# Offset attention in a two-layer decoder: outputs of two batches at a time, with gated mixtures kept in the buffer of the queries

## The chip, the cores and the metric

The kernel runs on one core of a Trainium2 chip. The metric is the device time of one execution in microseconds; of the kernel before there are three runs. TensorE is called PE here, VectorE DVE, ScalarE ACT, GpSimd POOL, and SyncE (which only starts transfers) SP.

## The reference

A decoder of two layers works on 16 batches of 112 tokens with 256 features: attention with future taps, cross attention, a mixture of experts, then offset attention, causal cross attention and a quantised perceptron. The change touches offset attention alone. Of the normalised input it makes queries, keys and values for 16 heads of 16 features, and for each allowed offset between query and key

```python
for i, o in enumerate(OFFSETS):
    qk = jnp.einsum('bhnd,bhnd->bhn', q, _shift(k, o))
    lg = qk * inv * (1.0 + qs[..., i]) + pos_bias[i][None, :, None]
    lg = jnp.where(pos[None, None, :] >= o, lg, NEG)
...
p = jax.nn.softmax(logits, axis=-1)
...
out = out * if_gain[None, :, None, None]
gate = jax.nn.sigmoid(x @ gate_w.T + gate_b)
return out_flat * gate @ out_w.T + out_b
```

The result is added to the residual stream `xT`. All arithmetic is float32.

## The kernel before

The stages follow each other, each with a block of instruction streams of its own, one per engine, written in the order in which they run; semaphores join them. The stage before this one left the queries of all batches in `qz_all` (`[P, 2, C, TOK]`: two variants, two halves, 1792 tokens), the gates in `gateT`, and the factors `1 + q . embedding` in DRAM.

`token_attention` (line 1352) serves three stages; in this one `offset` is true. Every engine loops over n = 0 to 17. Iteration n holds the front half of batch n and the back half of batches n-1 and n-2:

- PE (from line 1600): `scores(n)` (L1499), into PSUM banks 0 to 3; `turn(n-1, 0)` and `turn(n-1, 1)` (L1508), which transpose the probabilities; a norm's matmul (`beside.pe`, L256 or L273, bank 6) in iterations 7, 8, 11, 12, 15, 16; `turn` 2 and 3 and the products with the values, `mix` (L1523, bank 7); `values(n)` (L1471); `mix(n-1, 3)`; the keys of the next group of four batches (`project`, L1465) in iterations 1, 2, 5, 6, 9, 10, and those of the next stage (`project_cross`, L1578) in 13 to 15; then `output(n-2)` (L1539, bank 6).
- DVE (from line 1956): four `multiply` (L1851, scores times factors), the bias additions of two of the four groups of heads (L1856), a norm's centring (L261), four row maxima (L1863), the values (L1839), `spread_denominators(n-1)` (L1912), `add_output(n-2)` (L1922), then a norm's pair sum (L269), the queries of the next stage (L1831), a norm's scaling (L285) and sum (L252), where there are any.
- ACT (from line 1752): four copies of turned probabilities (L1721), the exponentials (L1727, eight small ones, and L1732, two large ones), `copy_mix(n-1)` (L1739) between them, keys (L1676), and the logarithm and exponential that invert the denominators (L1712, L1716).
- POOL (from line 2074): `normalise(n-2)` (L2040), two bias additions (L2045), two additions of the row maximum (L2050), `gate(n-1)` (L2032).
- SP fetches the factors of batch n when those of n-2 are used.

A mixture passes from bank 7 to `mixT` (ACT), times the gate to `gmixT` (POOL), times the inverted denominators in place (POOL), into the output's matmul (PE), and to `xT` with the bias (DVE). `mixT` and `gmixT` have two buffers here; the two other attention stages have four of `mixT` and already make the outputs of two batches at a time (`output_of_two`, L1548; `add_two`, L1945). Batches 14 and 15 go by `output_of_last` (L1557) in every stage. `x.after(At(n))` is the count that the semaphore x has after batch n; it starts four batches high, so that the first waits pass.

Of the kernel before, what the change touches and what calls it, by code (L numbers as in the profile page):

```python
# [12 lines left out]
ALU = mybir.AluOpType  # L13
# [3 lines left out]
P = 128  # L17
NB, T, D = 16, 112, 256
C = D // P
# [4 lines left out]
NG = H // HG  # L24
PADW = NG * P
FUT = 4
G = 448
# [1324 lines left out]
def token_attention(nc, kind, stage, psum, const, w, hT, accT, beside, ready, next_weights, ctxT=None, qz_all=None, gateT=None, skewed=None, startup=None, folded=None, big=None, spare=None, room=None, stored=None, perceptron=None, ups_ahead=None, weights=None, cross=None):  # L1352
# [9 lines left out]
    future, offset, causal = kind == "future", kind == "offset", kind == "causal"  # L1362
    ident, identb, maskb = const["ident"], const["identb"], const["maskb"]
    NV = 3 if future else 2
    with Scope(nc, stage, reuse=True) as s:
        NM = 2 if offset else 4
        mixT = qz_all[:, 0, 0].rearrange("p (u t) -> p u t", t=G) if causal else s.sb("mixT", [P, NM, G])
        if offset:
            gmixT = s.sb("gmixT", [P, 2, G])
        kT = cross.kT if causal else s.sb("kT", [P, 2, 2, G])  # L1370
# [4 lines left out]
        NR = 1 if offset else 2  # L1375
        rden = qz_all[:, 1, 0, 0:NR * G].rearrange("p (u t) -> p u t", u=NR) if causal else s.sb("rden", [P, NR, G])
        wt = w.at
# [32 lines left out]
        banks_free = factored if offset else shifted  # L1410
        out_mixT = gmixT if offset else mixT

# [40 lines left out]
        def _(pe):  # L1453
# [76 lines left out]

            def output(n):
                if offset:
                    pe.wait_ge(gained.sem, NG)
                beside.wait_bank(pe, n + 2)
                pe.wait_ge(*added.after(At(n - 1)))
                pe.wait_ge(*normed.after(At(n)))
                for m in range(C):
                    for g in range(NG):
                        mm = nc.tensor.matmul(psum[:, 6, m * T:(m + 1) * T], wt["wo"][:, g, m * P:(m + 1) * P], out_mixT[:, n % 2, g * T:(g + 1) * T], start=g == 0, stop=g == NG - 1)  # L1539
                mm.then_inc(projected.sem, 1)  # L1540

            def output_of_two(n):
                wait_norm_read(n + 1, n + 3)
                pe.wait_ge(*added.after(At(n // 2 - 1)))
                pe.wait_ge(*normed.after(At(n + 1)))
                for m in range(C):
                    for g in range(NG):
                        mm = nc.tensor.matmul(psum[:, 6, 2 * m * T:2 * (m + 1) * T], wt["wo"][:, g, m * P:(m + 1) * P], out_mixT[:, n % NM:n % NM + 2, g * T:(g + 1) * T], start=g == 0, stop=g == NG - 1)  # L1548
                mm.then_inc(projected.sem, 1)

            def output_of_last(n):

                bank = 4 + n % 2
                pe.wait_ge(*normed.after(At(n)))
                for m in range(C):
                    for g in range(NG):
                        mm = nc.tensor.matmul(psum[:, bank, m * T:(m + 1) * T], wt["wo"][:, g, m * P:(m + 1) * P], out_mixT[:, n % NM, g * T:(g + 1) * T], start=g == 0, stop=g == NG - 1)  # L1557
                mm.then_inc(projected.sem, 1)
# [41 lines left out]
            for n in range(NB + 2):  # L1600
# [18 lines left out]
                if beside.halves(n):  # L1619
                    pe.wait_ge(*added.after(At(n - 3 if offset else (n - 4) // 2)))  # L1620
                    beside.pe(pe, n, 6)
# [29 lines left out]
                if causal and n >= NB:  # L1651
                    for k in range(2):
                        pe.wait_ge(*shifted.after(At(NB - 1), 2 * (n - NB) + k))
                        weights.turn(pe, 2 * (n - NB) + k)
                if last and now and offset:
                    output(n - 2)
                elif n >= NB:
                    output_of_last(n - 2)
                elif not offset and n >= 3 and n % 2:
                    output_of_two(n - 3)  # L1660

        @block.scalar
        def _(act):
# [70 lines left out]
            def copy_mix(n):  # L1734
                if offset and n == 0:
                    act.wait_ge(*stored.after(At(NB - 1)))
                act.wait_ge(*mixed.after(At(n), NG - 1))
                act.wait_ge(*projected.after(At(n - 2 if offset else n // 2 - 2)))
                nc.scalar.copy(mixT[:, n % NM], psum[:, 7, 0:G]).then_inc(mix_copied.sem, 1)  # L1739
# [70 lines left out]
        def _(dve):  # L1810
# [102 lines left out]

            def add_output(n):
                dve.wait_ge(*projected.after(At(n)))
                if future:
                    x = accT[:, :, n * T:(n + 1) * T]
                    nc.vector.tensor_tensor(x, x, psum[:, 6, 0:C * T].rearrange("p (c t) -> p c t", c=C), ALU.add).then_inc(added.sem, 1)
                    return
                for c in range(C):  # L1920
                    x = accT[:, c, n * T:(n + 1) * T]
                    a = nc.vector.scalar_tensor_tensor(x, psum[:, 6, c * T:(c + 1) * T], wt["bo"][:, c:c + 1], x, ALU.add, ALU.add)  # L1922
                a.then_inc(added.sem, 1)

            def add_of_last(n):
                bank = 4 + n % 2
                dve.wait_ge(*(projected.after(At(n)) if offset else projected.after(At(NB // 2 - 1), n - (NB - 2))))
                if future:
                    x = accT[:, :, n * T:(n + 1) * T]
                    nc.vector.tensor_tensor(x, x, psum[:, bank, 0:C * T].rearrange("p (c t) -> p c t", c=C), ALU.add).then_inc(added.sem, 1)  # L1930
                    return
                for c in range(C):
                    x = accT[:, c, n * T:(n + 1) * T]
                    a = nc.vector.scalar_tensor_tensor(x, psum[:, bank, c * T:(c + 1) * T], wt["bo"][:, c:c + 1], x, ALU.add, ALU.add)
                a.then_inc(added.sem, 1)
# [20 lines left out]
            for n in range(NB + 2):  # L1956
# [43 lines left out]
                for name, g, m in pieces(n):  # L2000
                    if n < NB and name == "q":
                        take_queries(g, m, 5)
                if last and now and offset:
                    add_output(n - 2)
                    beside.dve_pair_now(dve, n)
                    if n in CROSS_AT and CROSS_AT[n][0] == "q":
                        take_cross_queries(CROSS_AT[n][1], 5)
# [5 lines left out]
                if offset and beside.sums(n):  # L2013
                    dve.wait_ge(*added.after(At(n - 2)))
                    beside.dve_sum(dve, n)

        @block.gpsimd
        def _(pool):
# [8 lines left out]
            def gate(n):  # L2027
                u = n % 2
                pool.wait_ge(*mix_copied.after(At(n)))
                pool.wait_ge(*projected.after(At(n - 2)))  # L2030
                m, gm = (x[:, u].rearrange("p (g t) -> p g t", g=NG) for x in (mixT, gmixT))
                nc.gpsimd.tensor_tensor(gm, m, gateT[:, :, n * T:(n + 1) * T], ALU.mult).then_inc(gated.sem, 1)  # L2032

            def normalise(n):
                u = n % 2
                if offset:
                    pool.wait_ge(*gated.after(At(n)))
                pool.wait_ge(*inverted.after(At(n)))
                x = out_mixT[:, n % NM]
                nc.gpsimd.tensor_tensor(x, x, rden[:, n % NR], ALU.mult).then_inc(normed.sem, 1)  # L2040

# [1156 lines left out]
```

## Time and profile before

| | us |
|---|---|
| median of 3 runs | 1714.85 (1712.42 to 1718.21) |
| the profiled execution | 1716.57 |
| its span | 1714.6 |
| PE busy | 1568.2 (91%) |
| DVE busy | 892.1 (52%) |
| ACT busy | 812.9 (47%) |
| POOL busy | 371.5 (22%) |
| offset attention | about 1329 to 1485 of the span |

Busy is the time in which the engine executes at least one instruction; the rest is waiting or issue. The shares are means over the whole span, and stages differ: over most of the span DVE, ACT and POOL wait for PE, and in offset attention all four are busy most of the time. A timeline row gives the start, the duration and the instruction, then in brackets how long the engine sat idle before it and whose instruction ended that wait; equal instructions that follow each other are merged to one row (x2). A shuffle (L1912) comes once in each iteration from 1 to 16, so the starts of its rows cut the stage into batches.

### The profile page before, as it was taken

The page shows a single profiled execution, that of the slowest core. Times are in us where ns is not written, and L with a number is a line of the kernel's source. Part 1 is how long each engine was busy: PE and PEld are TensorE (multiplying, and loading weights), DVE is VectorE, ACT ScalarE, POOL GpSimd, SP SyncE. Part 2 cuts the span into 40 slices and gives each one's busy share as a digit, 9 for nine tenths or more (in the row PEclk, how much of TensorE's full clock was granted, in tenths as well). Part 3 has the DMA queues.
Part 4 walks back from the last instruction along what each step waited for, and adds up shares of the span by engine and source line. Part 5 has one row for each costly group of instructions (what it writes and reads, how often), then busy time and mean ns, then how long its engine had stood idle before and what let it go on. Part 6 is the DMA issues. An engine that isn't in the chain of part 4 may idle for free. (4 is left out here: it accounts for less than half of the span.)

```text
span 1714.6 us, 34568 instructions
## 1 busy us (share of the span) xinstructions
PE 1568.2 (91%) x13646; PEld 1024.7 (60%) x13646; DVE 892.1 (52%) x1863; ACT 812.9 (47%) x1585; POOL 371.5 (22%) x337
## 2 busy tenths in 40 slices
PE   8899999999799999999799999999787899899965
PEld 3455555555356666656565999999344666566642
DVE  4566666511555565555242211111273889667758
ACT  4355555533144544455431222222254788556666
POOL 0012222221100010000028300000721777311222
PEclk9999999999899999999789999999999899999988
DMA  7000000010200000000043799997379443000001
GB/s 264 1 1 2 1 1 2 22 34 1 85 20 11 20 20 20 20 11 2 14 162 126 227 328 329 326 326 238 94 193 219 118 95 88 12 12 12 2 1 44
DMA packets 148051, 150.16 MB, mean 88 GB/s; under 512 B 69890, under 2 KB 135106, under 8 KB 147890
## 3 DMA queue, kind: packets, MB, share of 16 engines
q1 hardware_dynamic: 144818, 140.60, 26.9%
q0 software_dynamic: 3072, 7.34, 1.4%
q8 instruction: 109, 1.79, 0.5%
q14 instruction: 52, 0.43, 0.1%
HBM read 120.40 MB, written 27.53 MB: 86 GB/s over the span
## 5 line engine op out<-in xcount | busy, mean ns | idle before, releaser
L2506 DVE TENSOR_TENSOR masked<-masked 128x512 f32<-128x512 f32 x70 | 49.8, 712 | 200.9 <-ACT masked L2408 200.9
L958 DVE CUSTOM_DVE_ANT_0 x_unused<-psum,masked 112x439 f32<-112x439 f32 x256 | 141.8, 610 | 20.3 <-PE psum L781 19.6
L896 ACT ACTIVATE x_probs<-psum,key_mask 125x448 f32<-125x448 f32 x192 | 106.1, 635 | 77.4 <-PE psum L801 77.4
L2349 PEld LDWEIGHTS psum<-mix_xb,mix_up 128*128 128x128 f32 x1120 | 130.6, 192 | 2.1 <-issue 0.4
L2349 PE MATMUL psum<-mix_xb,mix_up 128*128 128x128 f32 x1120 | 130.7, 275 | 0.0
L2359 PE MATMUL psum<-mix_down,masked 128*128 128x256 f32 x560 | 127.0, 380 | 0.1
L1477 PE MATMUL psum<-fold_full,hT 128*112 128x512 f32 x256 | 113.8, 597 | 1.3 <-DVE fold_part L1872 1.3
L2359 PEld LDWEIGHTS psum<-mix_down,masked 128*128 128x128 f32 x560 | 103.5, 190 | 13.4 <-DVE masked L2506 0.4
L1721 ACT COPY masked<-psum 112x448 f32<-112x448 f32 x128 | 63.8, 530 | 60.6 <-PE psum L1508 60.3
L781 PE MATMUL psum<-x_kT,x_qz 32*112 32x439 f32 x512 | 88.4, 591 | 3.2 <-DVE x_kT L943 3.2
L2408 ACT ACTIVATE masked<-psum 128x512 f32<-128x512 f32 x70 | 41.8, 597 | 97.1 <-PE psum L2349 97.1
L1032 POOL TENSOR_TENSOR x_mixT<-x_mixT,x_rden 128x448 f32<-128x448 f32 x16 | 18.2, 1140 | 316.1 <-ACT x_rden L902 316.1
L801 PE MATMUL psum<-x_qmax,x_kT 32*125 32x112 f32 (+1 forms) x2048 | 81.4, 285 | 4.5 <-DVE x_qmax L966 3.8
L801 PEld LDWEIGHTS psum<-x_qmax,x_kT 32*125 32x125 f32 (+1 forms) x2048 | 66.7, 179 | 29.6 <-issue 20.8
L1508 PE MATMUL psum<-ident,second_result 112*112 112x112 f32 x512 | 70.2, 270 | 13.4 <-ACT masked L1721 9.4
L1477 PEld LDWEIGHTS psum<-fold_full,hT 128*112 128x112 f32 x256 | 44.1, 177 | 61.4 <-issue 58.9
L815 PEld LDWEIGHTS psum<-x_probs,x_v 125*32 125x32 f32 (+1 forms) x2048 | 47.5, 110 | 46.8 <-issue 26.3
L285 DVE TENSOR_TENSOR hT<-hT,sq 128x896 f32<-128x896 f32 x24 | 26.4, 1098 | 85.7 <-ACT sq L279 85.7
L1508 PEld LDWEIGHTS psum<-ident,second_result 112*112 112x112 f32 x512 | 50.9, 136 | 32.4 <-issue 23.6
L1115 POOL DMA_INDIRECT hrow<-slots_y,slot x16 | 15.6, 973 | 248.8 <-POOLq L148 245.3
L815 PE MATMUL psum<-x_probs,x_v 125*32 125x112 f32 (+1 forms) x2048 | 64.1, 264 | 4.7 <-ACT x_probs L896 4.6
L2414 ACT COPY mix_result<-psum 128x256 f32<-128x256 f32 x35 | 13.0, 372 | 99.1 <-PE psum L2359 99.1
(338 smaller groups left out, 3277.5 us busy)
## 6 DMA issues: line engine op xcount, KB each, us to landing
mix_up<-in_moe_up SPq DMA_DIRECT2D x35, 1024.0 KB
mix_down<-in_moe_down SPq DMA_DIRECT2D x35, 1024.0 KB
offset_rows<-join_rows SPq DMA_DIRECT2D x16, 784.0 KB, 5.7
hrow<-offset_rows SPq DMA_DIRECT2D x16, 784.0 KB, 5.2
x_ctx<-in_ctxT SPq DMA_DIRECT2D x16, 375.0 KB, 3.1
slots_x<-masked SPq DMA_DIRECT2D x1, 4480.0 KB, 21.4
mix_rows<-slots_x SPq DMA_DIRECT2D x35, 128.0 KB, 3.4
slots_y<-mix_result SPq DMA_DIRECT2D x35, 128.0 KB, 3.5
```

Source lines behind the costliest of these rows:

```text
L781: nc.tensor.matmul(psum[0:T, bank(*use), 0:KEYS], qz[rows, n // BATCHES_OF % 2, e, m, t:t + T], kT[rows, n % 3, m, e], start=True, stop=Tr ...
L801: mm = nc.tensor.matmul(psum[0:keys_of, bank(*use), k * T:(k + 1) * T], kT[rows, n % 3, m, e, c * CHUNK:c * CHUNK + keys_of], qmax[rows, k ...
L815: mm = nc.tensor.matmul(psum[32 * k:32 * k + 32, 7, g * T:(g + 1) * T], v[0:rows, n % 2, c, HG * g + k, :], probs[0:rows, 4 * (c % 2) + 2 ...
L896: nc.scalar.activation(probs[0:rows, 4 * (c % 2) + r], psum[0:rows, bank("tile", n, 4 * c + r), 0:G].rearrange("p (k t) -> p k t", k=4), A ...
L958: nc.vector.tensor_tensor_reduce(unused[:, at], psum[0:T, at, 0:KEYS], masked[0:T, n * KEYS:(n + 1) * KEYS], -1.0, -3.0 * NEG, ALU.add, AL ...
L1477: mm = nc.tensor.matmul(psum[0:T, bank, :], hT[:, c, n * T:(n + 1) * T], taps, start=c == 0, stop=c == C - 1)
L1508: mm = nc.tensor.transpose(psum[0:T, 4 + i % 2, k * T:(k + 1) * T], probs[:, n % 2, HG * i + k], ident[0:T, 0:T])
L1721: nc.scalar.copy(turned[:, i], psum[0:T, 4 + i % 2, 0:G].rearrange("p (k t) -> p k t", k=HG)).then_inc(copied.sem, 1)
L2349: mm = nc.tensor.matmul(psum[:, 2 * u + half, m * BLOCK:(m + 1) * BLOCK], e_up[:, w, c, (half * H4 + m) * P:(half * H4 + m + 1) * P], xb[: ...
L2359: mm = nc.tensor.matmul(psum[:, 6 + u, 0:D], e_hidden[:, u, m, :], e_down[:, w, m, :], start=m == 0, stop=m == M8 - 1)
L2408: nc.scalar.activation(e_relu[:, half], psum[:, 2 * (k % 2) + half, :].rearrange("p (m t) -> p m t", m=H4), ACT.Relu).then_inc(relu_done.s ...
L2506: nc.vector.tensor_tensor(e_hidden[:, u, half * H4:(half + 1) * H4], e_relu[:, half], e_relu[:, half], ALU.mult).then_inc(hidden_ready.sem, 1)
```

## The change

For the offset stage `NM`, the number of `mixT` buffers, goes from two to four. `gmixT` is no longer a buffer of its own: it is a view of `qz_all`, and the gated mixture of batch n takes the columns of the queries of batch n, once the scores of that batch are made. `output` and `add_output`, which did one batch in each iteration, are gone; `output_of_two` and `add_two` do two batches in odd iterations from 3 to 15. The waits follow: `copy_mix` waits for the gating and the shuffle of the batch four before, `gate` for the scores, and the norms' waits on `added` count pairs.

```diff
-        NM = 2 if offset else 4
+        NM = 4
...
-            gmixT = s.sb("gmixT", [P, 2, G])
+            gmixT = qz_all[:].rearrange("p e m t -> p (e m) t")
...
+        def mixed_heads(g, n, count):
+            if offset:
+                return gmixT[:, g, n * T:(n + count) * T]
+            return mixT[:, n % NM:n % NM + count, g * T:(g + 1) * T]
...
-            def output(n):
-                if offset:
+            def output_of_two(n):
+                if offset and n == 0:
                     pe.wait_ge(gained.sem, NG)
-                beside.wait_bank(pe, n + 2)
-                pe.wait_ge(*added.after(At(n - 1)))
-                pe.wait_ge(*normed.after(At(n)))
-                for m in range(C):
-                    for g in range(NG):
-                        mm = nc.tensor.matmul(psum[:, 6, m * T:(m + 1) * T], wt["wo"][:, g, m * P:(m + 1) * P], out_mixT[:, n % 2, g * T:(g + 1) * T], start=g == 0, stop=g == NG - 1)
-                mm.then_inc(projected.sem, 1)
-
-            def output_of_two(n):
                 wait_norm_read(n + 1, n + 3)
                 pe.wait_ge(*added.after(At(n // 2 - 1)))
                 pe.wait_ge(*normed.after(At(n + 1)))
                 for m in range(C):
                     for g in range(NG):
-                        mm = nc.tensor.matmul(psum[:, 6, 2 * m * T:2 * (m + 1) * T], ..., out_mixT[:, n % NM:n % NM + 2, g * T:(g + 1) * T], ...)
+                        mm = nc.tensor.matmul(psum[:, 6, 2 * m * T:2 * (m + 1) * T], ..., mixed_heads(g, n, 2), ...)
...
                 if beside.halves(n):
-                    pe.wait_ge(*added.after(At(n - 3 if offset else (n - 4) // 2)))
+                    pe.wait_ge(*added.after(At((n - 4) // 2)))
...
-                if last and now and offset:
-                    output(n - 2)
-                elif n >= NB:
+                if n >= NB:
                     output_of_last(n - 2)
-                elif not offset and n >= 3 and n % 2:
+                elif n >= 3 and n % 2:
                     output_of_two(n - 3)
...
                 act.wait_ge(*mixed.after(At(n), NG - 1))
-                act.wait_ge(*projected.after(At(n - 2 if offset else n // 2 - 2)))
+                if offset:
+                    act.wait_ge(*gated.after(At(n - NM)))
+                    act.wait_ge(*spread.after(At(n - NM)))
+                else:
+                    act.wait_ge(*projected.after(At(n // 2 - 2)))
...
+                if offset and now and n >= 3 and n % 2:
+                    add_two(n - 3)
                 if last and now and offset:
-                    add_output(n - 2)
                     beside.dve_pair_now(dve, n)
...
                 if offset and beside.sums(n):
-                    dve.wait_ge(*added.after(At(n - 2)))
+                    dve.wait_ge(*added.after(At((n - 3) // 2)))
...
             def gate(n):
-                u = n % 2
                 pool.wait_ge(*mix_copied.after(At(n)))
-                pool.wait_ge(*projected.after(At(n - 2)))
-                m, gm = (x[:, u].rearrange("p (g t) -> p g t", g=NG) for x in (mixT, gmixT))
+                pool.wait_ge(*scored.after(At(n), NG - 1))
+                m, gm = mixT[:, n % NM].rearrange("p (g t) -> p g t", g=NG), gmixT[:, :, n * T:(n + 1) * T]
                 nc.gpsimd.tensor_tensor(gm, m, gateT[:, :, n * T:(n + 1) * T], ALU.mult).then_inc(gated.sem, 1)
...
-                x = out_mixT[:, n % NM]
-                nc.gpsimd.tensor_tensor(x, x, rden[:, n % NR], ALU.mult).then_inc(normed.sem, 1)
+                x = gmixT[:, :, n * T:(n + 1) * T] if offset else mixT[:, n % NM]
+                nc.gpsimd.tensor_tensor(x, x, rden[:, n % NR].rearrange("p (g t) -> p g t", g=NG) if offset else rden[:, n % NR], ALU.mult).then_inc(normed.sem, 1)
```

The rest of the diff drops `add_output` and the counts of `projected` by single batches.

## Rows read from the trace of the kernel before

**Rows 1.** Windows view, the repeating part: us; busy (count) of PE, PEld, DVE, ACT, POOL; clock; DMA.

```profile
1350.89:1469.18 118.29, 108.09 (x1346) 79.78 (x1345) 106.01 (x207) 96.93 (x236) 91.05 (x79) 1.00 0.36 84
```

**Rows 2.** PE timeline, next stage (pairs): start us, us, instruction; a pair's output, its successor.

```profile
1518.41 3.19 PE L1548 MATMUL psum<-qz_all,weights 128*128 128x224 f32 x16
1521.43 0.92 PE L1493 MATMUL psum<-maskb,identb 112*112 112x448 bf16 x4
```

**Rows 3.** PE timeline, iterations 4 to 6, cut.

```profile
1363.03 0.56 PE L1508 MATMUL psum<-ident,second_result 112*112 112x112 f32 x4 [1.48 <-ACT masked L1721]
...
1375.55 1.93 PE L1539 MATMUL psum<-a_gmixT,weights 128*128 128x112 f32 x16
1377.42 1.05 PE L1499 MATMUL psum<-a_kT,qz_all 32*112 32x112 f32 x32
...
1379.87 0.57 PE L1508 MATMUL psum<-ident,second_result 112*112 112x112 f32 x4 [0.49 <-ACT masked L1721]
...
1383.12 1.77 PE L1465 MATMUL psum<-hT,weights 128*128 128x448 f32 x4
1384.73 1.93 PE L1539 MATMUL psum<-a_gmixT,weights 128*128 128x112 f32 x16
```

**Rows 4.** DVE timeline, offset attention, cut (L1912 STREAM_SHUFFLE opens each period).

```profile
1350.89 0.66 DVE L1912 STREAM_SHUFFLE a_rden<-a_mixT 128x448 f32<-128x448 f32 x1
...
1360.07 0.66 DVE L1912 STREAM_SHUFFLE a_rden<-a_mixT 128x448 f32<-128x448 f32 x1
...
1361.09 1.14 DVE L1851 SCALAR_TENSOR_TENSOR second_result<-hrow,psum 112x448 f32<-112x448 f32 x2
1362.15 0.62 DVE L1856 TENSOR_TENSOR second_result<-second_result,weights 112x448 f32<-112x448 f32 x1
...
1364.28 1.08 DVE L1856 TENSOR_TENSOR second_result<-second_result,weights 112x448 f32<-112x448 f32 x1
...
1367.73 0.66 DVE L1912 STREAM_SHUFFLE a_rden<-a_mixT 128x448 f32<-128x448 f32 x1
...
1376.38 0.66 DVE L1912 STREAM_SHUFFLE a_rden<-a_mixT 128x448 f32<-128x448 f32 x1
...
1378.49 1.15 DVE L1851 SCALAR_TENSOR_TENSOR second_result<-hrow,psum 112x448 f32<-112x448 f32 x2 [0.39 <-PE psum L1499]
1379.56 1.51 DVE L1856 TENSOR_TENSOR second_result<-second_result,weights 112x448 f32<-112x448 f32 x1
...
1385.56 0.66 DVE L1912 STREAM_SHUFFLE a_rden<-a_mixT 128x448 f32<-128x448 f32 x1
...
1387.31 0.63 DVE L252 TENSOR_TENSOR sq<-xT 128x448 f32<-128x448 f32 x1
...
1395.97 0.65 DVE L1912 STREAM_SHUFFLE a_rden<-a_mixT 128x448 f32<-128x448 f32 x1
...
1413.24 0.66 DVE L1912 STREAM_SHUFFLE a_rden<-a_mixT 128x448 f32<-128x448 f32 x1
...
1422.41 0.66 DVE L1912 STREAM_SHUFFLE a_rden<-a_mixT 128x448 f32<-128x448 f32 x1
...
1469.18 0.66 DVE L1912 STREAM_SHUFFLE a_rden<-a_mixT 128x448 f32<-128x448 f32 x1
...
1471.15 1.38 DVE L1831 TENSOR_SCALAR gateT<-psum,weights,half 128x448 f32<-128x448 f32 x2
```

**Rows 5.** POOL timeline, two rows of iterations 4 and 6.

```profile
1363.73 2.63 POOL L2045 TENSOR_TENSOR second_result<-second_result,weights 112x448 f32<-112x448 f32 x2
...
1379.45 1.14 POOL L2040 TENSOR_TENSOR a_gmixT<-a_gmixT,a_rden 128x448 f32<-128x448 f32 x1 [1.25 <-ACT a_rden L1716]
```

**Rows 6.** ACT timeline, iteration 4.

```profile
1364.92 2.35 ACT L1727 ACTIVATE second_result<-second_result,a_rowmax 112x112 f32<-112x112 f32 x8
```

**Rows 7.** Groups by line, 1335 to 1485: busy us, mean ns, idle before.

```profile
L1922 DVE SCALAR_TENSOR_TENSOR xT<-psum,weights,xT 128x112 f32<-128x112 f32 x28 | 8.0, 326 | 3.7 <-PE psum L1539 3.7
```

**Rows 8.** DVE timeline, next stage: the addition of a pair.

```profile
1521.63 0.81 DVE L1945 SCALAR_TENSOR_TENSOR xT<-psum,weights,xT 128x224 f32<-128x224 f32 x2 [3.76 <-PE psum L1548]
```

More of the change, by code:

```diff
@@ L1410, in token_attention @@
         banks_free = factored if offset else shifted
-        out_mixT = gmixT if offset else mixT
+        def mixed_heads(g, n, count):
+            if offset:
+                return gmixT[:, g, n * T:(n + count) * T]
+            return mixT[:, n % NM:n % NM + count, g * T:(g + 1) * T]
         def factor_load(sp, n):
@@ L1547, in output_of_two @@
                     for g in range(NG):
-                        mm = nc.tensor.matmul(psum[:, 6, 2 * m * T:2 * (m + 1) * T], wt["wo"][:, g, m * P:(m + 1) * P], out_mixT[:, n % NM:n % NM + 2, g * T:(g + 1) * T], start=g == 0, stop=g == NG - 1)
+                        mm = nc.tensor.matmul(psum[:, 6, 2 * m * T:2 * (m + 1) * T], wt["wo"][:, g, m * P:(m + 1) * P], mixed_heads(g, n, 2), start=g == 0, stop=g == NG - 1)
                 mm.then_inc(projected.sem, 1)
@@ L1556, in output_of_last @@
                     for g in range(NG):
-                        mm = nc.tensor.matmul(psum[:, bank, m * T:(m + 1) * T], wt["wo"][:, g, m * P:(m + 1) * P], out_mixT[:, n % NM, g * T:(g + 1) * T], start=g == 0, stop=g == NG - 1)
+                        mm = nc.tensor.matmul(psum[:, bank, m * T:(m + 1) * T], wt["wo"][:, g, m * P:(m + 1) * P], mixed_heads(g, n, 1), start=g == 0, stop=g == NG - 1)
                 mm.then_inc(projected.sem, 1)
@@ L1912, in spread_denominators @@
                 nc.vector.stream_shuffle(rden[:, n % NR], mixT[:, n % NM], [HD] * 32).then_inc(spread.sem, 1)
[L1914 to L1923, printed above, removed]
             def add_of_last(n):
                 bank = 4 + n % 2
-                dve.wait_ge(*(projected.after(At(n)) if offset else projected.after(At(NB // 2 - 1), n - (NB - 2))))
+                dve.wait_ge(*projected.after(At(NB // 2 - 1), n - (NB - 2)))
                 if future:
```

## The prediction

> **What bounds the kernel now.** I read the share of each engine first, then the stretches, then the timelines of offset attention. Only the part from the second to the last `stream_shuffle` of a denominator repeats: 118.29 us, with PE busy for 108.09 (91%), DVE 106.01 (90%), ACT 96.93 (82%), POOL 91.05 (77%) at full clock [rows 1]. The change touches one stage of 8% of the span, and no engine there has slack for all of a saving to be hidden or for all of it to be paid out. So the order within a batch decides, and I follow it from one shuffle (L1912) to the next. I call the stretch that the shuffle of iteration n opens period n, and give times in it from that shuffle's start.
>
> Periods last 9.18 us (n=2), 7.66 (3), 8.65 (4), 9.18 (5), 10.41 (6), 17.27 (7 and 8 together), 9.17 (9) and 46.76 (10 to 14) [rows 4]. They have a common form. Let m be the start of the first `multiply` (L1851). In period 3 it is 1.02, and the second L1856 took 1.08 us beside a POOL operation where the first, alone, took 0.62: 7.66 - 1.02 - 0.47 = 6.17. In period 5 m is 2.11 and the first L1856 took 1.51: 2.11 + 6.17 + 0.90 = 9.18 [rows 4]. So a period is m + 6.17 + what L1856 loses to POOL (+1.0 where a norm's centring is in it).
>
> Two things set m. DVE cannot start before the shuffle is issued, some 0.6; PE must have the scores: they start when the output ends, and L1851 follows 1.07 after their start (1377.42 to 1378.49) [rows 3, 4].
>
> There is a floor too. PE's third turn waits for an ACT copy, 2.96 into a period without keys (1363.03) and 3.49 into one with keys (1379.87) [rows 3]; the eight exponentials after it run without a gap in iteration 4 [rows 6], so ACT's chain ends 4.70 after that turn (1367.73 - 1363.03), and DVE's ends at the same time. A period is therefore not under 7.66, or 8.19 with keys. POOL's two bias additions, 2.63 us together [rows 5], are nearly as late.
>
> **The change, part by part.**
>
> *PE.* Fourteen outputs of one batch become seven of two. One takes 1.87 us to the next instruction (1375.55 to 1377.42) [rows 3]; one of two takes 3.02 (1518.41 to 1521.43) in the next stage, with equal shapes [rows 2]. Each pair saves 2 x 1.87 - 3.02 = 0.72 of PE, 5.0 us in seven. But it is no even saving: an even iteration loses 1.87 of PE work, an odd one gains 1.15, just ahead of the scores for which DVE waits.
>
> *DVE.* Two additions of some 0.57 become one of 0.81 per pair [rows 7, 8]. In odd periods it runs while PE computes the scores, in even ones DVE starts at 0.6 anyway; its 0.3 is inside m.
>
> *Even periods.* No output, so the scores are there before the shuffle and m falls to 0.6.
> - Period 2: POOL's L2040 stands at 3.07 with keys (1379.45) [rows 5], past the first L1856 at 1.7. The floor binds: 8.19 for 9.18, a gain of 0.99.
> - Period 4: the floor without keys, 7.66 for 8.65: 0.99.
> - Period 6: L252 stands before L1851, at 1.75 and 0.55 long [rows 4]. m falls from 2.30 to 1.15, and the L2040 that lengthened the first L1856 is now behind it, some 0.2: 1.37. Periods 10 and 14 have the same form: 1.37 each.
> - Periods 8 and 12: m is held by DVE's norm scale (about 1.1), and ends where it did: nothing.
>
> *Odd periods.* The output starts when the fourth mixture (and the keys) is through: 3.25 after the third turn (1379.87 to 1383.12), and 1.61 later with keys (to 1384.73) [rows 3]. m = its start + 3.02 + 1.07.
> - Period 3: the output starts at 3.49 + 3.25 - 8.19 = -1.45; m = 2.64; the period 8.81, no L1856 in POOL's way (POOL's bias addition then waits for the multiply): a loss of 1.15.
> - Period 5: 2.96 + 3.25 + 1.61 - 7.66 = +0.16; m = 4.25; 10.42: a loss of 1.24.
> - Periods 7 and 11: PE ends the output at about 0.7, DVE has the shuffle, the addition and a sum of squares to do until 2.2; the same first L1856 as now waits for L2040: under 0.1 of loss, taken as nothing.
> - Period 9: output from -0.9 to 2.15; m = 3.2; 9.39, for L1856 comes behind L2040 and no longer waits for it: a loss of 0.22. Period 13 comes to the same 9.39. Periods 10 to 14 last 46.76, and after the change by the above 9.04 + 17.27 + 9.39 + 9.04 = 44.74 (10 and 14 as period 6, 11 and 12 as 7 and 8, 13 as 9), a gain of 2.02.
>
> *The tail.* In iteration 15 DVE's cross queries end at 1471.15 + 1.38, 3.35 after the last shuffle [rows 4], and PE's next turn waits for them. With the output from -0.7 to 2.3, the addition of two, the sum of squares and the two L1831 behind it end at 5.3. Everything from there to the stage's end is one chain: a loss of 1.9. (If DVE's part stayed hidden it would be 0; it cannot be more than 3.02.)
>
> *Mixtures.* Four buffers instead of two, and `copy_mix` waits for POOL's gating and the shuffle of four batches ago instead of for an output: never late, before or after. POOL's gate now writes, and L2040 reads and writes, four runs of 112 with the stride of a row of `qz_all`. The gate reads `gateT` with that stride today; the trace has no strided write on POOL. The elements are the same, so it costs no less than 0; from above the nearest row is L2045, 1.31 each in a pair against L2040's 1.14 [rows 5]: 0.17 x 2 x 14 = 4.8 us if all of it were on the path. I take 0: a row of L2040 with a plain layout is the nearest, and it has slack before it. The gate's new wait, on scores of an iteration ago, is always met; behind it on POOL only the next normalisation stands. SP's loads wait for `factored` alone, and no DVE row waits for them here. The last output, now of batches 12 and 13, still needs the normalisation of 13 only.
>
> Sum: -0.99 (2) + 1.15 (3) - 0.99 (4) + 1.24 (5) - 1.37 (6) + 0 (7, 8) + 0.22 (9) - 2.02 (10 to 14) + 1.9 (tail) = **-0.9 us**. The profiled execution took 1716.57 (span 1714.6), so it becomes 1715.7; against the median of 1714.85 that is **1714.0**. A change under 0.3% (5.1 us) cannot be told from none here.
>
> **A rule to weigh.** L1856 has two inputs in SBUF and took 1.51 where POOL's L2040 had started 0.11 before it, and 0.62 alone [rows 4, 5]. The Trainium skill ("SBUF — State Buffer", section "SBUF: two separate sides") calls the ports that VectorE and GpSimd share an exclusive lock: who starts first has them for the whole instruction, the other fully blocks. The trace agrees for the loser on DVE's side (the row ends 0.48 after L2040 does). By this rule each L1856 whose start moves by a few tenths can turn from free to blocked, which is the second rival.
>
> **Rivals.**
> - *PE is the bound* (faster). If the odd periods' longer output were covered, PE's 5.0 us would come out whole: 1714.85 - 5.0 = 1709.8. For it: PE is the busiest engine and waits seldom [rows 1]. Against: DVE waits for scores right behind outputs, and the even iterations leave PE idle at ACT's copy [rows 3].
> - *POOL takes the port first in odd periods* (slower). With m late, POOL has long done L2040, and its two bias additions are released by DVE's second and fourth multiply, just as the two L1856 are issued behind them. If POOL were first, each L1856 would lose what the one of period 5 loses to L2040, 0.90. It decides from the point where L2045 starts before L1856, in periods 3, 5, 9 and 13, where nothing else is slack: 8 x 0.90 = 7.2, and 7.2 - 0.9 = +6.3: 1721.2. For it: both wait for the same multiply. Against: DVE issues L1856 without a wait (1362.15, right behind the two multiplies that began at 1361.09), and POOL has a semaphore to pass first [rows 4].
> - *The floor is higher* (same). If periods 2 and 4 kept their length (POOL's bias additions ending later as DVE comes to them earlier), 2.0 of the gain would be missing: 1716.0.
> - *The change does not do what it says:* with the output of two not at full rate, e.g. 2 x 1.87, odd periods would lose 0.7 more each, 1718; the next stage shows 3.02, so this has little.
>
> **How the numbers follow.** The forecast 0.63, the higher floor 0.14, PE as the bound 0.11, POOL's port 0.08, slow outputs or strided writes 0.04. Faster than 0.3%: the first rival, which lies at that edge and which I count there with what shorter L1856 would add, 0.11; slower: the second, 0.08; the same: 0.81. For the forecast alone 1712 to 1716. The range takes in the first rival and the strided writes (1714.0 + 4.8), and leaves out POOL's port: 1709.5 to 1719.
>
> **What would show it.** Periods must alternate: about 8.2, 8.8, 7.7, 10.4, 9.0, 9.0, 8.3, 9.4 for n = 2 to 9, where they now take 9.2, 7.7, 8.7, 9.2, 10.4, 17.3 for two, 9.2. L1548 in this stage 3.02 from start to successor, seven times; m of 0.6 in even periods, 2.6 and over in odd ones; DVE waiting for L1548 in odd periods only; the stage from the last shuffle to its end longer by 1.9. Wrong if even periods stay at 8.6 or more, if L1856 is long behind a pair's output, if L2040 or L2032 exceed 1.2, or if the total moves by over 5 us.

## The result, and the profile after

The changed kernel is slower. Against the kernel before on the same chip its time is a ratio of 1.0063 (95% interval 1.005 to 1.0076): 1729.36 us median of 15 runs against 1716.74 of 15, where 1714.0 and no measurable change were forecast. The profiled execution took 1726.35, its span is 1724.6 with PE busy for 1574.8 and a mean granted clock of 0.958 (before: 1714.6, 1568.2, 0.965). Chips differ by several microseconds, so whole times are compared below by the ratio to the kernel before on the same chip; periods come from the one profiled execution of each kernel. Three executions of the experiments, which took 1.5 to 5 times as long as the others of their kernel, are left out of the ratios.

Cut at the shuffles as before [rows 4], the stage gives:

| period n | 2 | 3 | 4 | 5 | 6 | 7 + 8 | 9 | 10 to 12 | 13 | 14 | 2 to 14 | 15 |
|---|---|---|---|---|---|---|---|---|---|---|---|---|
| before | 9.18 | 7.66 | 8.65 | 9.18 | 10.41 | 17.27 | 9.17 | 27.70 | 8.65 | 10.42 | 118.29 | 9.18 |
| predicted | 8.19 | 8.81 | 7.66 | 10.42 | 9.04 | 17.27 | 9.39 | 26.31 | 9.39 | 9.04 | 115.5 | |
| after | 9.01 | 9.76 | 9.45 | 11.62 | 10.42 | 17.28 | 10.96 | 28.40 | 11.53 | 10.42 | 128.85 | 11.32 |

(10 to 12 predicted: 9.04 + 17.27.) The repeating part is 10.6 us longer, period 15 another 2.1. What follows the last shuffle is 0.9 longer up to the start of the stage's last addition (6.16 for 5.28), and 2.4 up to the next stage's first operation on DVE (11.67 for 9.24). That makes some 15 us in this pair of traces, where the ratio gives 10.8 (8.6 to 13.0); the rest of the difference is not located. The spans differ by 10.0 only because the part ahead of the stage, which the change does not touch, was 5.2 us shorter in the execution after (the stage's first multiply starts at 1322.00 for 1327.16).

The first view to open is the windows view, here periods 2, 4, 5, 8, 12 and 13 of the kernel after: length, busy time and count of PE, PEld, DVE, ACT and POOL, then the granted clock, the DMA share and GB/s.

```profile
1346.06:1355.07 9.01, 6.96 (x71) 4.55 (x65) 6.97 (x15) 7.30 (x19) 7.30 (x7) 0.81 0.56 127
1364.83:1374.28 9.45, 7.19 (x53) 4.31 (x52) 7.36 (x13) 6.78 (x18) 7.36 (x7) 0.64 0.55 124
1374.28:1385.90 11.62, 11.29 (x109) 7.78 (x107) 7.29 (x15) 7.41 (x19) 6.29 (x6) 1.00 0.15 39
1405.27:1413.60 8.33, 5.98 (x50) 3.62 (x48) 7.96 (x16) 6.67 (x18) 6.44 (x7) 0.80 0.33 78
1443.93:1452.96 9.03, 6.68 (x48) 3.82 (x46) 8.04 (x14) 6.76 (x18) 7.16 (x7) 0.62 0.40 95
1452.96:1464.49 11.53, 11.20 (x109) 7.77 (x107) 7.28 (x15) 7.40 (x19) 6.29 (x6) 1.00 0.07 16
```

In the kernel before the clock of this whole part is 1.00 [rows 1]. Here it falls in four even periods (2, 4, 8 and 12), and again in period 15 (0.85). The PE timeline of the end of iteration 4 and of iteration 5 shows what PE did before, and what it costs:

```profile
1364.55 0.98 PE L1513 MATMUL psum<-ident,second_result 112*112 112x112 f32 x8 [0.38 <-DVE a_v L1837]
1367.80 0.97 PE L1513 MATMUL psum<-ident,second_result 112*112 112x112 f32 x4 [2.26 <-ACT masked L1715]
1368.69 0.60 PE L1528 MATMUL psum<-masked,a_v 112*32 112x112 f32 x8
1369.23 1.00 PE L1513 MATMUL psum<-ident,second_result 112*112 112x112 f32 x4
1370.15 0.98 PE L1528 MATMUL psum<-masked,a_v 112*32 112x112 f32 x16
1371.06 2.05 PE L1476 MATMUL psum<-weights,hT 128*112 128x256 f32 x4
1373.04 0.60 PE L1528 MATMUL psum<-masked,a_v 112*32 112x112 f32 x8
1373.57 2.12 PE L1470 MATMUL psum<-hT,weights 128*128 128x448 f32 x4
1375.53 3.19 PE L1544 MATMUL psum<-qz_all,weights 128*128 128x224 f32 x16
1378.65 1.05 PE L1504 MATMUL psum<-a_kT,qz_all 32*112 32x112 f32 x32
```

The same place in the kernel before, cut:

```profile
1370.69 0.57 PE L1508 MATMUL psum<-ident,second_result 112*112 112x112 f32 x4 [0.48 <-ACT masked L1721]
...
1372.57 1.12 PE L1471 MATMUL psum<-weights,hT 128*112 128x256 f32 x4
```

With no output in iteration 4, PE waits 2.26 us for ACT's copy, where the kernel before waited 0.48. Four transposes then take 0.97 (0.57 before) and the values 2.05 (1.12 before): about half the speed, the level of 1.2 GHz. The keys and with them the output start late, though the output itself takes 3.12 (1375.53 to 1378.65), near the 3.02 predicted. DVE waits at both ends, as its timeline shows for period 4's end and period 5:

```profile
1373.15 0.42 DVE L1837 TENSOR_TENSOR a_v<-psum,weights 112x256 f32<-112x256 f32 x1 [1.35 <-PE psum L1476]
...
1374.28 0.66 DVE L1910 STREAM_SHUFFLE a_rden<-a_mixT 128x448 f32<-128x448 f32 x1
1378.76 0.81 DVE L1932 SCALAR_TENSOR_TENSOR xT<-psum,weights,xT 128x224 f32<-128x224 f32 x2 [3.81 <-PE psum L1544]
1379.72 1.15 DVE L1849 SCALAR_TENSOR_TENSOR second_result<-hrow,psum 112x448 f32<-112x448 f32 x2 [0.15 <-PE psum L1504]
1380.79 0.62 DVE L1854 TENSOR_TENSOR second_result<-second_result,weights 112x448 f32<-112x448 f32 x1
```

m is 5.44 (1379.72 - 1374.28) instead of 4.25, and the first L1854 (the L1856 of before) is free, 0.62. So are both L1854 of periods 3, 9 and 13 (0.61 to 0.62): the second rival, POOL taking the port in odd periods, did not happen.

A second thing stands in periods 6, 10 and 14, which lost nothing and gained nothing. DVE and, below it, POOL of the kernel after, period 6:

```profile
1385.90 0.66 DVE L1910 STREAM_SHUFFLE a_rden<-a_mixT 128x448 f32<-128x448 f32 x1
1386.46 1.74 DVE L252 TENSOR_TENSOR sq<-xT 128x448 f32<-128x448 f32 x1
1388.12 1.14 DVE L1849 SCALAR_TENSOR_TENSOR second_result<-hrow,psum 112x448 f32<-112x448 f32 x2
1389.18 1.41 DVE L1854 TENSOR_TENSOR second_result<-second_result,weights 112x448 f32<-112x448 f32 x1
```

```profile
1386.57 1.14 POOL L2019 TENSOR_TENSOR qz_all<-a_mixT,gateT 128x448 f32<-128x448 f32 x1
1388.97 1.14 POOL L2027 TENSOR_TENSOR qz_all<-qz_all,a_rden 128x448 f32<-128x448 f32 x1 [1.26 <-ACT a_rden L1710]
```

L252 now follows the shuffle directly, meets POOL's gate (L2019) and takes 1.74 for the 0.63 of [rows 4]; then L1854 starts 0.21 behind L2027 and takes 1.41. Each ends 0.48 or 0.49 after the POOL operation does (1388.20 for 1387.71, 1390.59 for 1390.11). POOL's own operations keep their 1.14: the strided writes cost nothing that shows.

### The profile page after: what moved, and what is told of

The parts are those of the page before. It is cut to its first block and busy times, and to the rows that moved or that the text cites. A ratio compares the mean times of both kernels' runs of the same rounds, so it can differ in the third digit from the quotient of the medians.

```text
span 1724.6 us, 34321 instructions
## 1 busy us (share of the span) xinstructions
PE 1574.8 (91%) x13534; PEld 1023.6 (59%) x13534; DVE 890.7 (52%) x1849; ACT 811.8 (47%) x1585; POOL 370.8 (22%) x337
## 5 line engine op out<-in xcount | busy, mean ns | idle before, releaser
L2346 PEld LDWEIGHTS psum<-mix_down,masked 128*128 128x128 f32 x560 | 103.5, 190 | 13.3 <-DVE masked L2493 0.4
L1513 PE MATMUL psum<-ident,second_result 112*112 112x112 f32 x512 | 73.9, 278 | 21.0 <-ACT masked L1715 13.1
L1470 PE MATMUL psum<-hT,weights 128*128 128x448 f32 x120 | 55.1, 591 | 7.2 <-issue 4.4
```

Source lines behind the costliest of these rows:

```text
L1470: mm = nc.tensor.matmul(psum[:, bank, 0:G], wt["w" + name][:, c, m * P:(m + 1) * P], src, start=c == 0, stop=c == C - 1)
L1513: mm = nc.tensor.transpose(psum[0:T, 4 + i % 2, k * T:(k + 1) * T], probs[:, n % 2, HG * i + k], ident[0:T, 0:T])
L2346: mm = nc.tensor.matmul(psum[:, 6 + u, 0:D], e_hidden[:, u, m, :], e_down[:, w, m, :], start=m == 0, stop=m == M8 - 1)
```

## The experiments

Each was timed beside the kernel before, on the same chip. A filler below is a matmul whose result nobody reads.

**e1_buffers** takes the kernel before and changes only the buffers.

```diff
-        NM = 2 if offset else 4
+        NM = 4
-            gmixT = s.sb("gmixT", [P, 2, G])
+            gmixT = qz_all[:].rearrange("p e m t -> p (e m) t")
 ... the new waits of copy_mix and gate; output(n) and add_output(n) stay
```

> The kernel before with the new buffers alone: four mixT, the gated mixture in the columns of qz_all, the new waits; outputs still one batch in each iteration. My theory (the slowdown is from PE's idle time in even iterations and the slower clock that follows, and from DVE operations that now run into POOL's gate) expects the time of before, within 0.1%, clock 1.00 in the stage and periods of 7.7 to 10.4 us as before. If POOL's strided writes or the new waits cost, L2032 and L2040 exceed 1.14 us and the time is up to 5 us longer.

Ratio 1.0002 (0.9987 to 1.0017), and the repeating part 118.62 us for 118.29. The buffers and waits cost nothing that shows; the time is in the outputs' new order. One period of it (7) had a clock of 0.82 and 9.35 us, after a wait of 1.74 of PE; the kernel before has the same wait (1.73) and kept 1.00.

**e2_filler** gives PE something to do in its waits. (The wait for `gained` moves from the first output to a place ahead of the first fillers.)

```diff
+                    if offset and now and n in (3, 5, 9, 13):      # after turn(n - 1, 1)
+                        for k in range(4 if n == 3 else 8):
+                            nc.tensor.matmul(psum[:, 6, G:G + 64], wt["wo"][:, k % NG, 0:P], wt["wo"][:, k % NG, 0:64], start=True, stop=True)
```

> The changed kernel with matmuls of no use (64 columns into an unused part of bank 6) where PE waits for ACT's copies: four in iteration 3, eight in 5, 9 and 13. Clock theory: in the changed kernel's trace the granted clock is 0.81, 0.64, 0.80 and 0.62 in periods 2, 4, 8 and 12, after waits of 1.0 to 2.4 us, and matmuls take 1.8 times as long; with PE kept busy the clock stays near 1.00, periods 2 and 4 fall to about 8.2 and 7.7, 5, 9 and 13 to 10.4, 9.4 and 9.4, in all 6 to 9 us less than the changed kernel. Rival (the longer output just before the scores is the cost by itself): the clock may rise, but the total stays within 1 us of the changed kernel, or grows by what the fillers take (up to 1.7 us each in four places).

Ratio 1.0022 (1.0004 to 1.004) for 1.0063: two thirds of the loss are gone, though PE has more to do. The clock is 1.00 in periods 4 to 15, and periods 4, 5, 9 and 13 are 7.65, 10.54, 9.44 and 9.44 us (after: 9.45, 11.62, 10.96, 11.53; predicted: 7.66, 10.42, 9.39, 9.39). Period 2 kept a clock of 0.68 and took 9.88 us, where about 8.2 was expected: PE had waited 1.06 us ahead of these fillers, for ACT's keys.

**e5_filler_all** adds four fillers between the first two turns of iteration 3, and eight there in iteration 16, behind waits that keep them off a bank still being read.

```diff
                     turn(n - 1, 0)
+                    if offset and n == 3:
+                        pe.wait_ge(gained.sem, NG)
+                    if offset and n == NB and True:
+                        pe.wait_ge(*added.after(At(6)))
+                    if offset:
+                        for k in range({3: 4, NB: 8}.get(n, 0)):
+                            nc.tensor.matmul(psum[:, 6, G:G + 64], ...)
```

> The changed kernel with fillers where the clock still fell in e2_filler: in iteration 3 four between the first two turns (PE waits 1.06 us there for ACT's keys) and four after them, eight after the turns of 5, 9 and 13, and eight in iteration 16 between the first two turns (PE waits 2.8 us for DVE's queries). Clock theory: 1.00 in every period; 2 and 3 fall from 9.9 and 10.4 (e2_filler) to about 8.2 and 8.8 as the prediction had them, the rest stays as in e2_filler; 2 to 4 us below e2_filler, so within 0.1% of the kernel before. Rival (periods 2 and 3 are slow for another reason, a late start of the stage): the clock rises and they stay at 9.9 and 10.4.

Ratio 1.0016 (1.0003 to 1.003), where 0.1% at most was expected. Periods 2, 4, 5, 8, 12 and 13 in the windows view, to be read against the six rows of after:

```profile
1343.21:1351.38 8.17, 7.82 (x90) 6.23 (x85) 6.88 (x15) 7.20 (x19) 6.92 (x7) 1.00 0.63 142
1360.42:1368.06 7.64, 7.13 (x72) 5.23 (x71) 7.28 (x13) 6.67 (x18) 6.67 (x7) 1.00 0.57 139
1368.06:1378.61 10.55, 10.22 (x107) 7.21 (x105) 7.29 (x17) 7.42 (x19) 6.97 (x7) 1.00 0.22 53
1397.97:1406.30 8.33, 7.73 (x72) 5.64 (x70) 7.96 (x14) 6.78 (x18) 6.46 (x7) 1.00 0.34 81
1435.10:1443.42 8.32, 7.72 (x72) 5.63 (x70) 7.95 (x14) 6.77 (x18) 6.45 (x7) 1.00 0.33 79
1443.42:1452.88 9.46, 9.13 (x103) 6.30 (x101) 7.28 (x15) 7.42 (x19) 6.98 (x7) 1.00 0.17 39
```

The repeating part is 120.08 us: with the clock back, 8.8 of the 10.6 us are gone, although PE has more to do. Period 3 is 9.04 (predicted 8.81).

**e4_sum_later** moves L252 away from POOL's gate.

```diff
                     multiply(n, 0)
                     multiply(n, 2)
+                    if beside.sums(n - 1):
+                        dve.wait_ge(*added.after(At((n - 4) // 2)))
+                        beside.dve_sum(dve, n - 1)
 ...
-                if offset and beside.sums(n):
-                    dve.wait_ge(*added.after(At((n - 3) // 2)))
-                    beside.dve_sum(dve, n)
```

> The changed kernel with the norm's sum of iterations 6, 10 and 14 (L252 on DVE) moved behind the first two multiplies of the next iteration. Port theory: L252 takes 1.74 us right behind the shuffle because POOL's gate runs, 0.63 alone; moved it is 0.63 again, m falls from 2.2 to 0.6, and periods 6, 10 and 14 shrink by about 1.1 each, 3.3 us in all. Rival (those periods are bound by ACT and the norm's chain): L252 is short again, but the periods stay at 10.4 and the total within 1 us, or another DVE operation runs into POOL instead.

Ratio 1.0058 (1.0037 to 1.0079). The interval has room for the changed kernel's time and for the 3.3 us less that the port theory expected, so it decides neither. The windows of periods 6, 8 and 9 show more:

```profile
1391.11:1400.33 9.22, 8.49 (x99) 6.31 (x99) 8.09 (x15) 8.03 (x20) 6.96 (x7) 1.00 0.39 94
1409.65:1418.42 8.77, 6.42 (x48) 3.58 (x46) 7.97 (x16) 6.78 (x18) 6.86 (x6) 0.66 0.36 81
1418.42:1430.46 12.04, 11.71 (x108) 7.92 (x107) 7.28 (x15) 7.40 (x19) 6.43 (x7) 0.96 0.42 96
```

Period 6 lost its 1.2 us as the port theory had it (so did 10 and 14), and period 9 took 1.1 more than in the kernel after, behind a period 8 at 0.66 for 0.80. In all the repeating part was 126.23 us, 2.6 less than in the kernel after, but period 15 took 12.72 for 11.32.

**e6_filler_sum_later** is e5_filler_all with that edit.

> e5_filler_all with L252 behind the first two multiplies (the edit of e4_sum_later). In e4 periods 6, 10 and 14 fell from 10.42 to 9.23 but 7, 8, 9 rose, with a clock of 0.66 in period 8. If that was the clock, the 1.2 us of each now stay, the repeating part lasts about 117 us for 118.3 before, and the time is 3 us below e5_filler_all. If the time moved to the next periods for another reason (the norm's chain over DVE, ACT and PE), periods 7 and 8 stay longer at full clock, and the total equals e5_filler_all's.

Ratio 0.9996 (0.9984 to 1.0008), against 1.0016 for e5_filler_all on the same chip. The gain stays now. The same three periods:

```profile
1377.18:1386.41 9.23, 8.50 (x99) 6.32 (x99) 8.10 (x15) 8.04 (x20) 6.97 (x7) 1.00 0.39 97
1395.73:1403.97 8.24, 7.63 (x71) 5.55 (x70) 7.87 (x14) 6.77 (x18) 6.33 (x6) 1.00 0.30 73
1403.97:1413.50 9.53, 9.20 (x102) 6.37 (x100) 7.29 (x15) 7.41 (x19) 6.97 (x7) 1.00 0.59 134
```

The repeating part is 117.27 us, 2.8 less than e5_filler_all. The whole time is near what was forecast for the changed kernel (-0.04% measured, -0.05% predicted), but that is in part luck: the interval spans 4 us, this kernel has L252 elsewhere and 40 fillers, and its repeating part is 1.8 us over the 115.5 predicted (0.2 in each of periods 6, 10 and 14, 0.3 in 7 + 8 and in 11 + 12, 0.1 to 0.2 in each of 3, 5, 9 and 13).

**e9_narrow** issues the output of two batches in the old matmuls of 112 columns, everything else as after.

```diff
+                    for b in range(2 if offset else 1):
+                            to = psum[:, 6, (2 * m + b) * T:(2 * m + b + 1) * T] if offset else ...
+                            mm = nc.tensor.matmul(to, wt["wo"][:, g, m * P:(m + 1) * P], mixed_heads(g, n + b, 1), ...)
```

> The changed kernel with each output of two batches issued as matmuls of 112 columns (32 instructions of the old kind in the same place). It prices the saving of PE that the prediction put at 0.72 us per pair. If that term is right, an output takes 3.75 us instead of 3.02, and the odd periods in which DVE waits for it (3, 5, 9, 13) are 0.7 longer: 3 us more than the changed kernel, 12 to 14 over the one before. Rival (wide matmuls bring nothing): the changed kernel's time.

Ratio 1.0089 (1.0067 to 1.011). In iteration 7 the output takes 3.76 us to its successor, for 3.22 in the kernel after (1392.64 to 1395.86):

```profile
1390.18 3.83 PE L1546 MATMUL psum<-qz_all,weights 128*128 128x112 f32 x32
1393.94 1.05 PE L1504 MATMUL psum<-a_kT,qz_all 32*112 32x112 f32 x32
```

So the wide matmuls do save time, 0.54 per pair here for the 0.72 of the prediction. Period 9, behind a period 8 of the same length and clock (8.32 us, 0.79, for 8.33, 0.80), is 11.51 for 10.96, 0.55 longer. The repeating part is 132.32 us, 3.5 more than after; the clock differs too (0.68 in periods 2 and 4), so this sum is not the term's alone.

**e3_halves** keeps the wide matmuls but spreads them: iteration n makes one half of the features of a pair.

```diff
+            def half_output(i):
+                n, m = i - i % 2, i % 2
+                ...
+                pe.wait_ge(*added.after(At(i - 1)))
+                pe.wait_ge(*normed.after(At(n + 1)))
+                for g in range(NG):
+                    mm = nc.tensor.matmul(psum[:, 6, 2 * m * T:2 * (m + 1) * T], wt["wo"][:, g, m * P:(m + 1) * P], mixed_heads(g, n, 2), ...)
 ...
+                if offset and 3 <= n <= NB:
+                    half_output(n - 3)
-                elif n >= 3 and n % 2:
+                elif not offset and n >= 3 and n % 2:
```

> Outputs of two batches, but one half of the features per iteration: eight matmul instructions of 224 columns and one addition in each iteration from 3 to 16 instead of sixteen and two in odd ones. If the alternation (idle PE in even iterations, late scores in odd ones) is the cause, each iteration has 1.51 us of output for 1.87 before, no idle PE beyond that of before, clock 1.00, and the time is 2 to 5 us below the kernel before, 12 to 15 below the changed one. Rival (outputs of two or their operands are slow here whatever their order): close to the changed kernel.

Ratio 1.0013 (0.9999 to 1.0027). Most of the changed kernel's loss is gone, but not the gain I expected over the one before: this was a miss. Periods 4, 9 and 13 are 7.73, 8.40 and 8.41 (before 8.65, 9.17, 8.65), but iteration 2 is still without an output (periods 2 and 3 took 9.96 and 8.71, the clock of 2 was 0.67), and the fourteenth half came late in the tail, where the clock fell too: period 15 took 10.87 us and what follows, up to the last addition, 10.24, for 9.18 and 5.28.

**e7_halves_tail** mends both.

```diff
                     turn(n - 1, 0)
+                    if offset and n == NB:
+                        half_output(13)
+                    ... four fillers here and four after the second turn in iteration 3
```

> e3_halves (one half of the features of two batches in each iteration) with the fourteenth half in iteration 16 between the first two turns, where PE waits 2.8 us for DVE anyway, and eight fillers in iteration 3. In e3 the repeating part took 118.19 us, with 9.96 and 8.71 at a clock of 0.67 in periods 2 and 3, and the end of the stage 5 us more than before. With both mended: periods 2 and 3 about 8.2 and 7.8, the last ones as before, 3 to 4 us below the kernel before. Rival: the tail's cost was the additions' order on DVE, and remains; then the time is that of the kernel before.

Ratio 0.9996 (0.998 to 1.0012), short of the 0.2% expected, which the interval just reaches. Periods 2 and 3 are 8.17 and 8.35 and period 15 is 9.19, but now PE waits 1.73 us in iteration 5, period 4 has a clock of 0.80 (8.45, and 9.74 in period 5), and after the last shuffle an output at half the clock makes it 6.90 us.

**e8_halves_sum_later** adds the move of L252.

> e7_halves_tail with L252 behind the first two multiplies of the next iteration. Port theory: periods 6, 10 and 14 are 1.0 to 1.2 us shorter as in e4, 3 us less than e7_halves_tail. Clock theory adds that it holds only if PE's waits in iterations 8 and 9 do not grow over those of e7 (1.7 and 1.0 us); otherwise periods 7 to 9 give it back.

Ratio 1.002 (1.0011 to 1.0029): slower, against my expectation. The multiplies begin later here (the scores wait for a half output), so L252 lands on POOL's normalisation. DVE and POOL, period 6:

```profile
1379.21 1.15 DVE L1870 SCALAR_TENSOR_TENSOR second_result<-hrow,psum 112x448 f32<-112x448 f32 x2 [0.51 <-PE psum L1504]
1380.28 1.04 DVE L252 TENSOR_TENSOR sq<-xT 128x448 f32<-128x448 f32 x1
1381.24 1.55 DVE L1875 TENSOR_TENSOR second_result<-second_result,weights 112x448 f32<-112x448 f32 x1
```

```profile
1379.69 1.14 POOL L2055 TENSOR_TENSOR qz_all<-qz_all,a_rden 128x448 f32<-128x448 f32 x1 [1.26 <-ACT a_rden L1731]
1380.80 1.51 POOL L2060 TENSOR_TENSOR second_result<-second_result,weights 112x448 f32<-112x448 f32 x1
```

Periods 6, 10 and 14 are 11.89 for 10.41. The same edit that gave 1.2 us in e6 costs 1.5 here.

**e11_halves_filler** is e7_halves_tail with eight fillers more in iteration 5 and eight before the last output.

> e7_halves_tail with eight more fillers in iteration 5 (behind a wait for the second half's addition), where PE waited 1.73 us and period 4 ran at a clock of 0.80 (8.45 and 9.74 us in periods 4 and 5, against 7.73 and 9.18 in e3_halves), and eight before the very last output, which ran at half the clock (3.66 us for 2.04). Clock theory: periods 4 and 5 are 7.7 and 9.2 again, the part after the last shuffle 5.3 for 6.9; together 2 to 3 us below e7_halves_tail, 0.1 to 0.2% below the kernel before. Rival: the fillers cost as much as the clock gives back, and the time is that of e7_halves_tail.

Ratio 0.9966 (0.9951 to 0.9981), faster than both kernels: 5.8 us (3.3 to 8.4) less than before. The gain over e7_halves_tail was expected at 2 to 3 us; the ratios differ by 0.3%, with intervals that leave room for that. Periods 4 and 5, now 7.64 and 9.17, and the end, 5.29, are as expected, and the repeating part is 116.26 us. Period 7 lies at a clock of 0.82 in it, so something may still be left. The trace does not account for the whole gain: from the stage's first multiply to the next stage's first operation on DVE it shows 159.17 us for 160.44 in the kernel before, 1.3 less. Where the rest comes from is not shown.

## Why the prediction was wrong

- *What bounds the stage.* "m + 6.17 + what L1856 loses", the floor and the alternation were right as long as the clock is full. At full clock (e5_filler_all) periods 2, 3, 4, 5, 9 and 13 came at 8.17, 9.04, 7.64, 10.55, 9.44 and 9.46, where 8.19, 8.81, 7.66, 10.42, 9.39 and 9.39 were predicted.
- *PE's output.* 3.02 for 2 x 1.87: nearly right. After, it took 3.12 behind keys and 3.22 without; in e9_narrow 3.65 and 3.76, so the saving is 0.53 to 0.54 per pair against matmuls of 112 columns in the same place.
- *The step that failed: even periods.* "No output, so the scores are there before the shuffle": true, and left at that. That PE then stands idle at ACT's copy is said under the first rival, but nothing was put down for what the idle time does to the clock. PE waits 2.26 us at the ACT copy in iteration 5, 2.35 in 9 and 13, two waits of about 1.0 in 3, and behind each of these places the clock was at 1.2 GHz, at once or about 1 us later. The floor shows it in its own terms: PE's third turn comes 2.97 into period 4 (1367.80), as it did before into period 3, but the next shuffle comes 6.48 behind it (1374.28), not 4.70. Every duration in the sum had been taken from rows at full clock, which held for the kernel before and not for the one after. Shown by e2_filler and e5_filler_all: 8.8 of the 10.6 us of the repeating part. Against the 115.5 predicted for it the miss is 13.3: these 8.8, 4.1 in periods 6, 10 and 14 (next point), and 0.4 elsewhere.
- *Period 6, 10, 14.* "m falls from 2.30 to 1.15" for a gain of 1.37: mis-sized, it was nothing. I watched the POOL operation that L1856 would meet and not the one that L252 would, POOL's gate directly behind the shuffle. Moved away from it, each period is 9.23 (e6_filler_sum_later), a gain of 1.18.
- *The tail.* 1.9 predicted; period 15 and what follows up to the last addition are 3.0 longer after (4.6 up to the next stage's first operation on DVE). The clock fell here too: behind a wait of 2.36 the matmuls of L1574 took 2.31 for 1.68. In e5_filler_all, with period 15 at full clock, it is 0.8 (9.63 + 5.62), in e6_filler_sum_later 1.85 (11.03 + 5.28). There period 14 is 9.23, near the 9.04 that the prediction had ahead of the tail.
- *Mixtures.* Nothing that shows, as predicted (e1_buffers: 1.0002, 0.9987 to 1.0017).
- *The rule on the shared ports.* It was written down for L1856 and should have been held against every DVE operation with two inputs in SBUF that moved. That who starts first keeps the port fits L1854, which started 0.21 behind L2027 and took longer. It does not show for L252, whose record starts 0.11 before the gate's and which took longer all the same; but a DVE record often starts some 0.1 before the one ahead of it ends (1386.46 for 1386.56 here), so who was first is not settled.
- *The rivals.* All were priced at full clock; none contained what happened. The sign of the outcome was given 0.08, for another mechanism.

What stays open: what makes the clock fall. Behind the waits of 2.3 us at ACT's copy in iterations 5, 9 and 13 it always did (the kernel after, e4_sum_later, e9_narrow). But in iteration 16, where PE waits for DVE's queries, the kernel before waits longer than that and its matmuls stay fast, while the changed kernel's do not:

```profile
1472.59 0.60 PE L1508 MATMUL psum<-ident,second_result 112*112 112x112 f32 x4 [2.54 <-DVE gateT L1831]
1473.03 1.68 PE L1578 MATMUL psum<-hT,weights 128*128 128x448 f32 x4
```

```profile
1478.77 0.59 PE L1513 MATMUL psum<-ident,second_result 112*112 112x112 f32 x4 [2.36 <-DVE gateT L1829]
1479.21 2.31 PE L1574 MATMUL psum<-hT,weights 128*128 128x448 f32 x4
```

e2_filler waits 2.36 there as well and keeps its clock at 1.00. Behind 1.7 the clock fell in e1_buffers and e11_halves_filler (period 7) and in e7_halves_tail (period 4), and did not in the kernel before (iteration 8) nor in e3_halves at 1.74. So the length of one wait does not decide alone, and I ran nothing that shows what does.

## What to carry to other kernels

Before counting work taken from PE as a gain, follow what PE does in the freed time: if it becomes a wait, like the 2.3 us here, price the matmuls behind it at half the clock as well as at full, and look at the granted clock of each stretch before trusting durations. Work that is saved in bursts leaves gaps and piles up elsewhere. The same saving in pairs made this kernel slower (1.0063); spread evenly over the iterations it came near the time of before (e3_halves, 1.0013), and spread with 24 fillers in the waits that were left it was faster (e11_halves_filler, 0.9966). A DVE operation with two SBUF inputs that is moved, even to an idle place, has to be laid beside POOL's timeline at its new place.

## What the runs showed of the hardware

Matmuls of no use made the changed kernel faster (1.0063 to 1.0016): 40 calls, placed in waits, kept the clock at 1.00 in the periods where it had been 0.62 to 0.81 (8.8 us of 129), and left periods 4, 5, 9 and 13 within 0.13 of the lengths predicted without them (e5_filler_all). The granted clock fell behind a wait of 2.36 us of PE in one kernel and stayed at 1.00 behind 2.54 in another, at the same place of the program. A DVE operation with two inputs in SBUF that POOL blocked ended 0.48 or 0.49 after POOL's did: L252 took 1.74 for 0.63 where POOL's 1.14 began with it, L1854 1.41 for 0.62 where POOL's began 0.21 earlier.
